# A recommendation kernel's dense layers moved to its start, and its last tile cut into four units of 32 samples

## The chip, the cores and the metric

The kernel runs on one NeuronCore of one Trainium2 chip. The metric is the device time of one execution in microseconds (us). The kernel is written engine by engine: TensorE (PE), VectorE (DVE), ScalarE (ACT), GpSimd (POOL) and SyncE (SP) each have a program of their own, in the order in which it is written, and meet only at semaphores.

## What is computed

For 2048 samples, 26 embedding rows of 64 floats and one dense feature are multiplied pairwise; the 351 products and a small network on the price feed a top layer of 256 units and one output.

```python
emb = emb_tables[jnp.arange(NUM_FIELDS)[:, None], x_cat]        # 26 x 2048 rows of 64
emb = jnp.transpose(emb, (1, 0, 2))
dense_embed = price[:, None] @ Wp + bp
feats = jnp.concatenate([emb, dense_embed[:, None, :]], axis=1)  # 27 features
gram = jnp.einsum('bid,bjd->bij', feats, feats)
interactions = gram[:, _IU, _JU]
h = jax.nn.relu(dense_embed @ W1 + b1)
dense_out = jax.nn.relu(h @ W2 + b2)
concat = jnp.concatenate([interactions, dense_out], axis=1)
t = jax.nn.relu(concat @ Wt1 + bt1)
out = (t @ Wt2 + bt2)[:, 0]
```

Everything is float32.

## The kernel before

The samples are cut into 16 tiles of 128. For each tile POOL issues 26 gathers (`gather`, L200), one for each field: each fetches 128 rows of 256 bytes into `gathered`, which has room for one tile, so that a gather of tile t+1 into a chunk of the columns waits until PE has transposed that chunk of tile t (`chunk_transposed`). There are two chunks, of 14 and 12 fields.

PE transposes pairs of fields into `ps_trans` (`transpose_fields`, L419). DVE and ACT copy the halves into `feats` (`evacuate_chunk`, L151), 64 samples on the upper 64 partitions and 64 on the lower. The products of four samples at a time are one matmul of 128 columns (`gram_matmuls`, L456), issued for both halves in turn; a tile has 32 of them, in two rounds of 16. DVE and ACT copy out of `ps_gram` what is wanted of a round (`evacuate_gram`, L141), 8 copies each. Where the profile counts instructions, each of these float32 matmuls and its weight load is two.

Tiles form batches: four of four tiles at most, here (0,4), (4,8), (8,12), (12,14), (14,15), (15,16). At the first tile of a batch PE also does the two dense layers for it (`hidden_layer` L441, `dense_out_layer` L446), and the top layer of the batch before (`top_layer`): for each of its two halves m one matmul from `dense_out` (L479) and seven from `gram` (L487), then the score (`score`, L495).

The last tile has transposes in four chunks of fields, (0,8), (8,16), (16,24), (24,26), and products in four rounds of eight matmuls. Its indices are laid out so that the first two rounds need only the first two chunks and the other two need all. After the last gather there come thus one transpose, its copies, two rounds of products, their copies, and the top layer of 128 samples. `keep_warm` (L402) issues matmuls whose result nobody reads, while PE waits.

The order of work is the order in which each engine's program is written: PE's last steps are `transpose_last`, `gram_last`, `top_layer`, `score`. An instruction that waits holds up all that is written behind it on the same engine.

Of the kernel before, what the change touches and what calls it, by code (L numbers as in the profile page):

```python
# [7 lines left out]
BM1, BM2, TM1 = 128, 64, 256  # L8
P = 128
# [6 lines left out]
UNITS = 2  # L16
UNIT = HALF // UNITS
# [9 lines left out]
LAST_CHUNKS = [(0, 8), (8, 16), (16, 24), (24, 26)]  # L27
LAST_ROUNDS = 4
LAST_RG = GROUPS // LAST_ROUNDS

BATCHES = [(0, 4), (4, 8), (8, 12), (12, 14), (14, 15), (15, 16)]
# [3 lines left out]
WARM = (0, 7, 3, 1, 1)  # L35
TO_GRAM, TO_TOP = 4, 5
# [9 lines left out]
def rec_kernel(nc, price, x_cat, table, consts, w1, w2, wt1_pairs, wt1_dense, out):  # L46
# [3 lines left out]
    with ExitStack() as ctx:  # L50
# [12 lines left out]
        last_base = sb("last_base", [P, FIELDS], i32)  # L63
# [11 lines left out]
        dense = sb("dense", [D, WIDE * P])  # L75
        hidden = sb("hidden", [BM1, WIDE * P])
        dense_out = sb("dense_out", [BM2, WIDE * P])
# [25 lines left out]
        last_gathered = [sem(f"last_gathered{c}") for c in range(len(LAST_CHUNKS))]  # L103
        chunk_transposed = [sem(f"chunk_transposed{c}") for c in range(NC)]
        last_transposed = sem("last_transposed")
# [12 lines left out]
        top_made = sem("top_made")  # L118
# [8 lines left out]
        last_from = ps_gram[:, :].rearrange("p (r h g s j c) -> p r h g s j c", r=2, h=2, g=LAST_RG, s=GROUP,  # L127
# [5 lines left out]

        def evacuate_gram(copy, t, r, quads):

            n = batch_of[t]
            rg = LAST_RG if t == LAST else RG
            source = last_from[:, r % 2] if t == LAST else gram_from
            for s in quads:
                for c in range(GROUP):  # L140
                    last = copy(gram_to[QUAD * c:QUAD * (c + 1), n % 2, t - BATCHES[n][0], :, rg * r:rg * (r + 1), :, s],  # L141
                                source[QUAD * s:QUAD * (s + 1), :, :, s, 0:SLABS, c])
            return last
# [10 lines left out]
        def evacuate_unit_chunk(copy, c, kk):  # L154

            f0, f1 = LAST_CHUNKS[c]
            src = ps_trans[:, BANK * (c % 2):BANK * (c % 2 + 1)].rearrange("p (m q h b) -> p m q h b", m=BANK // P, q=2, h=2)
            for u in range(UNITS):
                slots = [s for s in range(f0 + kk, f1, 2) if s // (FIELDS // 2) == u]
                if not slots:  # L160
                    continue
                m0, n, f = (slots[0] - f0) // 2, len(slots), 1 + 2 * (slots[0] % (FIELDS // 2))
                for h in range(2):
                    dst = feats[D * h:D * (h + 1), UNIT * u:UNIT * (u + 1), f:f + 4 * n]
                    dst = dst.rearrange("p b (m r) -> p m r b", r=4)[:, :, 0:2, :]
                    last = copy(dst, src[D * kk:D * (kk + 1), m0:m0 + n, :, h, :])  # L166
            return last

# [3 lines left out]
        def _(sp):  # L172
# [5 lines left out]
            sp.wait_ge(score_stored, len(BATCHES))  # L178
# [4 lines left out]
        def _(pool):  # L183

            pool.iota(field_base[:, :], pattern=[[VOCAB, FIELDS]], base=0, channel_multiplier=0).then_inc(base_made, 1)

            for q in range(2):

                pool.wait_ge(base_made, q + 1)
                pool.iota(last_base[HALF * q:HALF * (q + 1), :], pattern=[[0, UNITS], [2 * VOCAB, FIELDS // 2]],  # L190
                          base=q * VOCAB, channel_multiplier=0).then_inc(base_made, 1)
            pool.wait_ge(base_made, 3)
# [11 lines left out]
            for t in range(LAST):  # L204
                if t == 0:
                    pool.wait_ge(rows_made, 1)
                else:
                    pool.wait_ge(rows_made, 3)
# [379 lines left out]
```

## Time and profile before

| | |
|---|---|
| median of 3 runs | 541.97 us (541.65 to 544.13) |
| the profiled execution: time | 542.15 us |
| the profiled execution: span, first to last instruction | 540.3 us |
| POOL busy | 393.8 us, 73% of the span |
| PE busy | 246.3 us, 46% |
| ACT busy | 169.1 us, 31% |
| DVE busy | 145.4 us, 27% |
| mean granted TensorE clock | 0.70 of full speed |

The profiled execution is 0.18 us longer than the median; 1.85 us of its time lie outside the span. Busy time of POOL is that of the gathers' own instructions; between two of them lies a part that the profile calls "issue", in which the engine waits for nothing that the profile shows. The granted clock is 1.0 or 0.5 of 2.4 GHz in any stretch, so a number between them is a mean over both.

### The profile page before, as it was taken

Reading aid. Unit: us, or ns where it says so; the run is one execution under the profiler, and the core shown is the slowest. Engines: PE = TensorE matmul, PEld = TensorE weight load, DVE = VectorE, ACT = ScalarE, POOL = GpSimd, SP = SyncE. Lnnn points to the kernel's source line nnn. Section 1 sums busy time; section 2 is a strip of 40 time slices with the busy share of each in tenths; the row PEclk is TensorE's granted clock in tenths of the full one; section 3 lists DMA queues with packets and bytes.
Section 4 is the critical chain, followed back from the end, with each engine's and each line's share of the span. In section 5 each row is a group of like instructions: output and inputs, shape, how many; then the busy total and the mean of one; then the engine's idle time right before and its main releaser. Section 6 shows DMA issues by size and latency. Waiting matters only on the chain.

```text
span 540.3 us, 4362 instructions
## 1 busy us (share of the span) xinstructions
PE 246.3 (46%) x1496; PEld 177.9 (33%) x1496; DVE 145.4 (27%) x358; ACT 169.1 (31%) x405; POOL 393.8 (73%) x425
## 2 busy tenths in 40 slices
PE   0118033240569515134249733315136960565775
PEld 0105033240534304133234423305134440544654
DVE  3003233040331504123040331503233051333353
ACT  0124323041241604223042440503224052243563
POOL 6777777777777777777777777777777777777750
PEclk9999665555659856555577975755555985669798
DMA  6233333333323333333333333333332333332210
GB/s 187 26 26 27 26 28 27 26 27 27 26 27 27 26 27 28 26 26 27 26 29 26 27 27 26 27 27 27 26 27 26 26 28 26 26 28 27 28 22 2
DMA packets 14360, 16.26 MB, mean 30 GB/s; under 512 B 7169, under 2 KB 7425, under 8 KB 14209
## 3 DMA queue, kind: packets, MB, share of 16 engines
q0 software_dynamic: 13312, 13.66, 30.9%
q1 hardware_dynamic: 578, 2.19, 1.1%
q8 instruction: 12, 0.20, 0.1%
q10 hardware_dynamic: 448, 0.14, 0.1%
q14 instruction: 10, 0.08, 0.0%
HBM read 15.95 MB, written 0.01 MB: 30 GB/s over the span
## 4 chain that ended last, share of the span: by engine, by line
POOL 68%; issue 26%; DMA 2%; PE 2%; ACT 1%; DVE 0%; POOLq 0%
POOL gathered L200 68%; DMA gathered<-in_table,row_idx 2%; PE ps_mlp L487 1%; ACT gram L141 1%; PE ps_trans L419 1%; DMA raw_idx<-in_x_cat 0%; POOLq L50 0%; PE ps_gram L456 0%; PE ps_mlp L479 0%; PE ps_mlp L495 0%; DVE feats L166 0%; DVE top L368 0%; ACT scores L279 0%; DVE row_idx L339 0%; DVE wrapped L332 0%
## 5 line engine op out<-in xcount | busy, mean ns | idle before, releaser
L200 POOL DMA_INDIRECT gathered<-in_table,row_idx x416 | 392.7, 944 | 128.0 <-issue 125.9
L419 PE MATMUL ps_trans<-ident,gathered 128*128 128x128 f32 x208 | 45.4, 381 | 223.0 <-DMA gathered<-in_table,row_idx 223.0
L456 PE MATMUL ps_gram<-feats 64*128 64x128 f32 x1024 | 105.2, 384 | 61.0 <-ACT gram L141 30.2
L141 ACT COPY gram<-ps_gram 32x112 f32<-32x112 f32 (+1 forms) x272 | 97.2, 357 | 108.1 <-PE ps_gram L456 105.2
L141 DVE COPY gram<-ps_gram 32x112 f32<-32x112 f32 (+1 forms) x272 | 96.6, 355 | 116.8 <-PE ps_gram L456 113.5
L456 PEld LDWEIGHTS ps_gram<-feats 64*128 64x128 f32 x1024 | 96.9, 286 | 75.4 <-issue 52.6
L419 PEld LDWEIGHTS ps_trans<-ident,gathered 128*128 128x128 f32 x208 | 35.0, 198 | 236.3 <-issue 234.9
L151 ACT COPY feats<-ps_trans 64x448 f32<-64x448 f32 (+1 forms) x60 | 34.1, 569 | 195.4 <-PE ps_trans L419 195.0
L151 DVE COPY feats<-ps_trans 64x448 f32<-64x448 f32 (+1 forms) x60 | 36.8, 613 | 203.3 <-PE ps_trans L419 202.7
L487 PE MATMUL ps_mlp<-gram,wt1p_sb 128*128 128x512 f32 (+2 forms) x168 | 60.2, 520 | 2.9 <-ACT gram L141 2.9
L487 PEld LDWEIGHTS ps_mlp<-gram,wt1p_sb 128*128 128x128 f32 x168 | 32.6, 228 | 32.6 <-issue 28.0
L368 DVE TENSOR_SCALAR top<-ps_mlp,consts_sb 128x512 f32<-128x512 f32 (+2 forms) x6 | 3.4, 574 | 66.7 <-PE ps_mlp L487 66.7
L237 ACT ACTIVATE feats<-price_bc,consts_sb 64x64 f32<-64x64 f32 x32 | 15.6, 488 | 0.7
L479 PE MATMUL ps_mlp<-dense_out,wt1d_sb 64*128 64x512 f32 (+2 forms) x24 | 13.9, 672 | 2.0 <-ACT dense_out L269 2.0
L274 ACT ACTIVATE top<-ps_mlp,consts_sb 128x512 f32<-128x512 f32 (+2 forms) x6 | 3.3, 545 | 27.0 <-PE ps_mlp L487 27.0
L151 ACT ACT_TABLE_LOAD x1 | 1.3, 1283 | 25.4 <-PE ps_trans L419 25.4
L495 PE MATMUL ps_mlp<-top,consts_sb 128*1 128x512 f32 (+2 forms) x24 | 7.9, 449 | 1.0 <-DVE top L368 1.0
L479 PEld LDWEIGHTS ps_mlp<-dense_out,wt1d_sb 64*128 64x128 f32 x24 | 4.8, 247 | 6.7 <-issue 4.4
L446 PE MATMUL ps_mlp<-hidden,w_sb 128*64 128x512 f32 (+2 forms) x12 | 6.6, 644 | 0.5 <-ACT hidden L264 0.5
L441 PE MATMUL ps_mlp<-dense,w_sb 64*128 64x512 f32 (+2 forms) x12 | 5.4, 532 | 1.5 <-ACT scores L279 1.5
L402 PE MATMUL ps_trans<-wt1p_sb,ident 128*128 128x256 f32 x24 | 6.1, 388 | 0.0
L166 ACT COPY feats<-ps_trans 64x256 f32<-64x256 f32 (+2 forms) x10 | 4.5, 450 | 4.5 <-PE ps_trans L419 4.4
(24 smaller groups left out, 33.5 us busy)
## 6 DMA issues: line engine op xcount, KB each, us to landing
gathered<-in_table,row_idx POOLq DMA_INDIRECT x416, 3.3
price_bc<-in_price SPq DMA_DIRECT2D x1, 1024.0 KB, 5.2
wt1p_sb<-in_wt_pairs SPq DMA_DIRECT2D x1, 896.0 KB, 7.8
raw_idx<-in_x_cat SPq DMA_DIRECT2D x1, 195.0 KB, 2.7
w_sb<-in_w ACTq DMA_DIRECT2D x2, 32.0 KB, 4.8
wt1d_sb<-in_wt_dense ACTq DMA_DIRECT2D x1, 64.0 KB, 7.7
raw_idx<-in_x_cat SPq DMA_DIRECT2D x1, 13.0 KB, 1.8
consts_sb<-in_consts ACTq DMA_DIRECT2D x1, 4.5 KB, 2.0
```

Of the source, the lines that this page charges most:

```text
L141: last = copy(gram_to[QUAD * c:QUAD * (c + 1), n % 2, t - BATCHES[n][0], :, rg * r:rg * (r + 1), :, s], source[QUAD * s:QUAD * (s + 1), :, ...
L151: last = copy(feats[D * h:D * (h + 1), :, 1 + f0 + q:f1 + q:2], src[D * q:D * (q + 1), h, :, :])
L200: pool.indirect_dma_start(out=gathered[:, to * D:(to + 1) * D], out_offset=None, in_=rows, in_offset=bass.IndirectOffsetOnAxis(ap=row_idx[ ...
L237: return nc.scalar.activation(dst, price_bc[part, first:first + n], ACT.Identity, bias=const(BP, part), scale=const(WP, part))
L402: nc.tensor.matmul(ps_trans[:, BANK * bank:BANK * bank + TM1], ident[:, :], wt1p_sb[:, 0:TM1], start=True, stop=True)
L419: last = nc.tensor.transpose(ps_trans[:, to + k * P:to + (k + 1) * P], gathered[:, base + f * D:base + (f + 2) * D], ident[:, :])
L441: nc.tensor.matmul(ps_mlp[0][:, 0:width(n)], w1_sb[:, :], dense[:, 0:width(n)], start=True, stop=True)\
L446: nc.tensor.matmul(ps_mlp[1][0:BM2, 0:width(n)], w2_sb[:, :], hidden[:, 0:width(n)], start=True, stop=True)\
L456: last = nc.tensor.matmul(ps_gram[:, out_at:out_at + P], group, group, start=True, stop=True)
L479: nc.tensor.matmul(ps_mlp[m][:, 0:w], wt1d_sb[:, m * P:(m + 1) * P], dense_out[:, 0:w], start=True, stop=False)
L487: last = nc.tensor.matmul(ps_mlp[m][:, 0:w], wt1p_sb[:, j * TM1 + m * P:j * TM1 + (m + 1) * P], gram[:, at:at + w], start=False, stop=(j = ...
L495: last = nc.tensor.matmul(ps_mlp[0][0:1, 0:width(n)], const(WT2 + m), top[m][:, 0:width(n)], start=(m == 0), stop=(m == 1))
```

## The change

- The two dense layers are computed for all 2048 samples ahead of tile 0, in four steps of 512 columns, into a `dense_out` that now holds them all.
- The batches are (0,4), (4,8), (8,12), (12,14), (14,16). Tile 14 has its products in four rounds of eight matmuls.
- The last tile is gathered in four units of 32 samples and all 26 fields, in place of chunks of fields. A gather still fetches 128 rows; it now takes four fields for 32 samples (six such gathers a unit), and two further gathers carry the last two fields of two units each. So a unit has 7, 6, 7 and 6 gathers. Its transposes, copies and round of products follow unit by unit.
- The top layer of the last batch (256 columns) is in two parts: 224 columns (`EARLY`) that don't need the last unit, and 32 columns that do and that sum in `ps_trans`. The two sums of 224 columns are written before and after the last unit.
- There are 2 and 6 `keep_warm` matmuls before the second and third unit, none after; before there were 7, 3, 1 and 1.
- The base row numbers of the last tile are no longer made by POOL; DVE makes the last tile's indices in 12 small additions, in place of one.

```diff
-BATCHES = [(0, 4), (4, 8), (8, 12), (12, 14), (14, 15), (15, 16)]
+BATCHES = [(0, 4), (4, 8), (8, 12), (12, 14), (14, 16)]
+DENSE = BATCH // BANK
...
-WARM = (0, 7, 3, 1, 1)
+WARM = (2, 6, 0)
...
+        def last_part(m, late):
+
+            if not late:
+                return slice(0, EARLY), ps_mlp[m][:, 0:EARLY]
+            return slice(EARLY, 2 * P), ps_trans[:, BANK * m:BANK * m + UNIT]
...
+            pool.wait_ge(rows_made, 2 + 3 * UNITS)
             pool.wait_ge(chunk_transposed[0], LAST)
-            for c, (f0, f1) in enumerate(LAST_CHUNKS):
-                if c == 1:
+            for n in range(UNITS):
+                if n == 2:
                     pool.wait_ge(chunk_transposed[1], LAST)
-                for f in range(f0, f1):
-                    gather(LAST, f, last_gathered[c])
+                for col in UNIT_COLS[n]:
+                    gather(LAST, col, unit_gathered[n])
...
+            for q in range(UNITS):
+                part = slice(UNIT * q, UNIT * (q + 1))
...
+            def even_unit(n):
+                dve.wait_ge(unit_transposed, n + 1)
+                if n % 2 == 0:
+                    evacuate_shared(nc.vector.tensor_copy, n)
+                evacuate_unit(nc.vector.tensor_copy, n, 0).then_inc(trans_evac_dve, 1)
...
+            def top_sums(n, m, part, to, rounds):
+
+                a, first = BATCHES[n][0] * P, (n % 2) * SLABS * WIDE * P
+                nc.tensor.matmul(to, wt1d_sb[:, m * P:(m + 1) * P], dense_out[:, a + part.start:a + part.stop],
+                                 start=True, stop=False)
+                wait_gram_evac(rounds)
+                for j in range(SLABS):
+                    at = first + j * WIDE * P
+                    last = nc.tensor.matmul(to, wt1p_sb[:, j * TM1 + m * P:j * TM1 + (m + 1) * P],
+                                            gram[:, at + part.start:at + part.stop], start=False, stop=(j == SLABS - 1))
+                last.then_inc(top_summed[m], 1)
...
+            transpose_unit(0)
+            transpose_unit(1)
+            fine_round(LAST, 0)
+            fine_round(LAST, 1)
+            transpose_unit(2)
+            fine_round(LAST, 2)
+            top_part(0, 0)
+            transpose_unit(3)
+            fine_round(LAST, 3)
+            top_part(1, 0)
+            for m in range(2):
+                top_part(m, 1)
+            for late in range(2):
+                score_part(late)
```

PE's program at its end, before, from the transposes of fields 16 to 23 of the last tile on (L419 transposes, L402 `keep_warm`, L456 products, L479 and L487 top layer, L495 score; a matmul is counted once here):

```order
L419 MATMUL ps_trans<-ident,gathered 128x128 x4
L402 MATMUL ps_trans<-wt1p_sb,ident 128x256 x3
L419 MATMUL ps_trans<-ident,gathered 128x128
L402 MATMUL ps_trans<-wt1p_sb,ident 128x256
L456 MATMUL ps_gram<-feats 128x128 x16
L479 MATMUL ps_mlp<-dense_out,wt1d_sb 128x128
L402 MATMUL ps_trans<-wt1p_sb,ident 128x256
L487 MATMUL ps_mlp<-gram,wt1p_sb 128x128 x7
L479 MATMUL ps_mlp<-dense_out,wt1d_sb 128x128
L487 MATMUL ps_mlp<-gram,wt1p_sb 128x128 x7
L495 MATMUL ps_mlp<-top,consts_sb 1x128 x2
```

And now, from the third unit's product round on (L491 transposes, L538 products, L544 and L549 top layer, L579 score):

```order
L538 MATMUL ps_gram<-feats 128x128 x8
L544 MATMUL ps_mlp<-dense_out,wt1d_sb 128x224
L549 MATMUL ps_mlp<-gram,wt1p_sb 128x224 x7
L491 MATMUL ps_trans<-ident,gathered 128x128 x3
L538 MATMUL ps_gram<-feats 128x128 x8
L544 MATMUL ps_mlp<-dense_out,wt1d_sb 128x224
L549 MATMUL ps_mlp<-gram,wt1p_sb 128x224 x7
L544 MATMUL ps_trans<-dense_out,wt1d_sb 128x32
L549 MATMUL ps_trans<-gram,wt1p_sb 128x32 x7
L544 MATMUL ps_trans<-dense_out,wt1d_sb 128x32
L549 MATMUL ps_trans<-gram,wt1p_sb 128x32 x7
L579 MATMUL ps_mlp<-top,consts_sb 1x224 x2
```

One product round of eight stands behind the last transposes in place of two, and one half of the wide top layer stands ahead of them; behind the last products there are now three groups of top-layer matmuls and a fourth of the same kind, in place of two, and two scores in place of one.

ACT's program at its start, before (L237 makes dense features, L151 copies tile 0's transposes, L264 and L269 are the dense layers' rectifiers):

```order
L151 COPY feats<-ps_trans 64x64x7 x2
L237 ACTIVATE dense<-price_bc,consts_sb 64x512
L237 ACTIVATE feats<-price_bc,consts_sb 64x64 x2
L151 COPY feats<-ps_trans 64x64x6 x2
L141 COPY gram<-ps_gram 32x2x8x7 x8
L264 ACTIVATE hidden<-ps_mlp,consts_sb 128x512
L141 COPY gram<-ps_gram 32x2x8x7 x8
L269 ACTIVATE dense_out<-ps_mlp,consts_sb 64x512
```

And now (L258 dense features, L291 and L295 the rectifiers, L166 the copies of tile 0's transposes):

```order
L258 ACTIVATE dense<-price_bc,consts_sb 64x512
L291 ACTIVATE hidden<-ps_mlp,consts_sb 128x512
L258 ACTIVATE dense<-price_bc,consts_sb 64x512
L295 ACTIVATE dense_out<-ps_mlp,consts_sb 64x512
L291 ACTIVATE hidden<-ps_mlp,consts_sb 128x512
L258 ACTIVATE dense<-price_bc,consts_sb 64x512
L295 ACTIVATE dense_out<-ps_mlp,consts_sb 64x512
L291 ACTIVATE hidden<-ps_mlp,consts_sb 128x512
L258 ACTIVATE dense<-price_bc,consts_sb 64x512
L295 ACTIVATE dense_out<-ps_mlp,consts_sb 64x512
L291 ACTIVATE hidden<-ps_mlp,consts_sb 128x512
L295 ACTIVATE dense_out<-ps_mlp,consts_sb 64x512
```

All four steps of the dense layers now precede the first copy of tile 0.

## Rows read from the trace of the kernel before

**Rows 1.** The page: two groups of instructions; busy us, mean ns, idle before, releaser.

```profile
L200 POOL DMA_INDIRECT gathered<-in_table,row_idx x416 | 392.7, 944 | 128.0 <-issue 125.9
...
L151 ACT ACT_TABLE_LOAD x1 | 1.3, 1283 | 25.4 <-PE ps_trans L419 25.4
```

**Rows 2.** Timeline, the start: start, duration (us), instruction, idle before it.

```profile
3.71 1.11 POOL L200 DMA_INDIRECT gathered<-in_table,row_idx  x1 [1.56 <-DVE row_idx L339]
...
5.80 0.18 DVE L348 TENSOR_TENSOR row_idx<-clamped,last_base 128x26 uint32<-128x26 f32 x1
6.35 1.76 DVE L350 MEMSET feats<- 128x2048 f32 x1 [0.37 <-issue]
...
23.61 1.73 PE L419 MATMUL ps_trans<-ident,gathered 128*128 128x128 f32 x7 [23.61 <-DMA gathered<-in_table,row_idx]
...
41.46 3.78 PE L456 MATMUL ps_gram<-feats 64*128 64x128 f32 x32 [1.30 <-DVE feats L151]
45.03 1.91 PE L441 MATMUL ps_mlp<-dense,w_sb 64*128 64x512 f32 x2
...
48.45 0.69 ACT L264 ACTIVATE hidden<-ps_mlp,consts_sb 128x512 f32<-128x512 f32 x1
```

**Rows 3.** Timeline of the tail, from the last gathers to the end.

```profile
514.43 0.94 POOL L200 DMA_INDIRECT gathered<-in_table,row_idx  x1 [0.30 <-issue]
...
521.92 0.94 POOL L200 DMA_INDIRECT gathered<-in_table,row_idx  x1 [0.30 <-issue]
...
522.18 0.66 PE L419 MATMUL ps_trans<-ident,gathered 128*128 128x128 f32 x4
...
522.87 1.25 DVE L166 COPY feats<-ps_trans 64x256 f32<-64x256 f32 x2 [0.41 <-PE ps_trans L419]
...
524.78 0.33 PE L419 MATMUL ps_trans<-ident,gathered 128*128 128x128 f32 x1 [0.65 <-DMA gathered<-in_table,row_idx]
...
525.79 2.06 PE L456 MATMUL ps_gram<-feats 64*128 64x128 f32 x32 [0.25 <-DVE feats L166]
526.99 4.41 DVE L141 COPY gram<-ps_gram 32x56 f32<-32x56 f32 x16 [1.30 <-PE ps_gram L456]
...
527.54 0.30 PEld L479 LDWEIGHTS ps_mlp<-dense_out,wt1d_sb 64*128 64x128 f32 x2
...
531.56 2.64 PE L487 MATMUL ps_mlp<-gram,wt1p_sb 128*128 128x128 f32 x14 [2.89 <-ACT gram L141]
...
534.85 2.23 PE L487 MATMUL ps_mlp<-gram,wt1p_sb 128*128 128x128 f32 x14
...
537.53 0.60 PE L495 MATMUL ps_mlp<-top,consts_sb 128*1 128x128 f32 x4 [0.45 <-DVE top L368]
538.16 0.36 ACT L279 ACTIVATE scores<-ps_mlp,consts_sb 1x128 f32<-1x128 f32 x1 [3.56 <-PE ps_mlp L495]
```

**Rows 4.** Groups by shape: busy us, mean ns of one.

```profile
L166 DVE COPY feats<-ps_trans 64x192 f32<-64x192 f32 x2 | 1.0, 484 | 0.1
L166 DVE COPY feats<-ps_trans 64x64 f32<-64x64 f32 x4 | 1.1, 266 | 1.1 <-PE ps_trans L419 1.0
```

**Rows 5.** Timeline at 480 to 490 us: a top layer of 256 columns.

```profile
480.94 5.04 PE L487 MATMUL ps_mlp<-gram,wt1p_sb 128*128 128x256 f32 x14
...
486.54 3.29 PE L487 MATMUL ps_mlp<-gram,wt1p_sb 128*128 128x256 f32 x14
```

**Rows 6.** Stretches: us, PE, PEld, DVE, ACT, POOL busy, PEclk, DMA share, GB/s.

```profile
478.00:484.00 6.00, 5.87 (x16) 4.38 (x17) 1.26 (x2) 2.63 (x5) 4.54 (x5) 0.50 0.35 30
484.50:490.00 5.50, 5.33 (x23) 3.83 (x21) 0.14 (x1) 0.47 (x1) 4.28 (x5) 1.00 0.38 28
...
528.00:530.00 2.00, 0.67 (x3) 0.26 (x2) 1.88 (x9) 1.90 (x9) 0.00 (x0) 1.00 0.00 0
...
532.50:535.50 3.00, 3.00 (x13) 2.55 (x13) 0.00 (x0) 0.37 (x1) 0.00 (x0) 0.50 0.00 0
```

**Rows 7.** Weight loads at 527.3 to 527.9 us, by shape: busy us, mean ns.

```profile
L479 PEld LDWEIGHTS ps_mlp<-dense_out,wt1d_sb 64*128 64x128 f32 x2 | 0.3, 188 | 0.0
```

More of the change, by code:

```diff
@@ L274, in top_relu, with part_relu @@
                 nc.scalar.activation(top[0][:, 0:width(n)], ps_mlp[0][:, 0:width(n)], ACT.Relu, bias=const(BT1))\
-                    .then_inc(top_made, 1)
+                    .then_inc(top_made[0], 1)
+            def part_relu(late):
+                part, sums = last_part(0, late)
+                act.wait_ge(top_summed[0], last_batch + 1 + late)
+                nc.scalar.activation(top[0][:, part], sums, ACT.Relu, bias=const(BT1)).then_inc(top_made[0], 1)
             def store_scores(n):
@@ L280, in store_scores, with store_part @@
                                      ACT.Identity, bias=const(BT2, slice(0, 1))).then_inc(score_stored, 1)
+            def store_part(late):
+                part, _ = last_part(0, late)
+                first = BATCHES[last_batch][0] * P
+                act.wait_ge(score_summed, last_batch + 1 + late)
+                nc.scalar.activation(scores[:, first + part.start:first + part.stop],
+                                     ps_mlp[late][0:1, 0:part.stop - part.start],
+                                     ACT.Identity, bias=const(BT2, slice(0, 1))).then_inc(score_stored, 1)
@@ L282, in _ @@
+            dense_batch(0)
+            for k in range(DENSE):
+                hidden_relu(k)
+                if k + 1 < DENSE:
+                    dense_batch(k + 1)
+                dense_out_relu(k)
             for t in range(LAST):
                 n = batch_of[t]
-                first = t == BATCHES[n][0]
+                first = t == BATCHES[n][0] and n > 0
                 odd_fields(0, t)
+                dense_slots(t)
                 if first:
-                    dense_batch(n)
@@ L497, in score, with score_part @@
                 last.then_inc(score_summed, 1)
+            def score_part(late):
+                part, _ = last_part(0, late)
+                for m in range(2):
+                    pe.wait_ge(top_made[m], last_batch + 1 + late)
+                    last = nc.tensor.matmul(ps_mlp[late][0:1, 0:part.stop - part.start], const(WT2 + m), top[m][:, part],
+                                            start=(m == 0), stop=(m == 1))
+                last.then_inc(score_summed, 1)
+            for k in range(DENSE):
+                hidden_layer(k)
+                dense_out_layer(k)
@@ L528, in _ @@
-            top_layer(n)
-            score(n)
+                if t < LAST - 1:
+                    gram_round(t, 0)
+                    gram_round(t, 1)
+                else:
+                    for r in range(FINE_ROUNDS):
+                        fine_round(t, r)
+            transpose_unit(0)
[6 more added lines that the diff above has]
+            transpose_unit(3)
@@ L567 @@
     idx = cat.transpose(2, 1, 0).copy()
[L568 removed]
+    last = cat[:, -1].reshape(FIELDS, UNITS, 2, SIDE)
+    own = last[:SHARED].reshape(COLS, UNITS, UNITS, 2, SIDE).transpose(1, 3, 4, 2, 0).reshape(P, UNITS, COLS)
+    shared = last[SHARED:].reshape(2, 2, 2, 2, SIDE).transpose(2, 0, 3, 4, 1).reshape(P, 2)
+    for n in range(UNITS):
+        idx[:, -1, UNIT_COLS[n][0]:UNIT_COLS[n][0] + COLS] = own[:, n]
+        if n % 2 == 0:
+            idx[:, -1, UNIT_COLS[n][COLS]] = shared[:, n // 2]
     idx = idx.reshape(P, TILES * FIELDS)
```

319 lines of the change are left out of this document (162 added, 157 removed).

## The prediction

> **What bounds the kernel now.** I read the chain that ended last, which runs through POOL's gathers for nearly the whole span, and then their group on the page: 392.7 us busy and 125.9 us of "issue" ahead of the 416 gathers, out of 128.0 us idle [rows 1]. Of the 2.1 us that are left, 1.56 are the wait ahead of the first one [rows 2]. So POOL never waits for another engine in a way that counts: the first gather starts at 3.71, the last at 521.92 [rows 2, 3], which is 518.21 us over 415 steps, 1.249 us each. No work of the other engines inside that stretch costs anything unless it holds up a gather.
>
> Then I read the tail. The last data are there when PE starts the last transpose, at 524.78, 2.86 us after the last gather's start. From there to the end of the span, 540.3, are 15.5 us, and they are one chain: copies, two product rounds of eight from 525.79, their copies from 526.99 for 4.41 us, the top layer's two sums from 531.56 and 534.85, scores, the store [rows 3]. The reader should see in these rows that PE, DVE and ACT take turns. This tail is what the change can alter.
>
> The third view is the granted clock. PE was busy 0.67 of the 2.0 us from 528, then steadily from 531.56, and the clock reads 0.50 in 532.5 to 535.5. The other way round, it was busy 5.87 of 6 us at 0.50, and then the clock reads 1.00 [rows 6]. These two levels are 1.2 and 2.4 GHz.
>
> **What stays.** There are 416 gathers before and after, each of 128 rows; I take 1.249 us for each. The first waits for the same DVE result. Hence the last data again at 524.8.
>
> **The dense layers at the start.** ACT begins them when `feats` is zeroed. The twelve additions stand ahead of that; the one that they replace took 0.18 us, and at as much each the memset of 1.76 us starts near 8.3 instead of 6.35, and ends at 10.1 [rows 2]. Then the table load, 1.3 us [rows 1], and one activation, some 0.8. A step is two matmuls of 1.91 us, a rectifier of 0.69 and two more matmuls that I take at the same 1.9 [rows 2]: 4.5 us, four of them 18.0. That ends at 30.2. The transposes of tile 0 stood at 23.61 and took 1.73 us; they move to about 30.2 and end at 31.9. The first gather that needs them is the 27th, at 3.71 + 26 x 1.249 = 36.2. There are 4.3 us in hand, so the cost is nothing. Beyond 36.2 each us would be a us of the total. Their removal from later tiles, from between product rounds, gains nothing either, as POOL is the bound there.
>
> **Tile 14 in four rounds.** Its copies are four rounds of eight copies an engine at 4.41/16 = 0.276 us [rows 3], 8.8 us. They must be done before those of the second unit, whose last gather is 13 steps, 16.2 us, behind that of tile 14. That cover holds with 7 us to spare. No POOL wait hangs on it.
>
> **The third unit.** Its last gather is the one of 514.43, six steps ahead of the last [rows 3]; with 2.86 us its data are there at 517.3. The six `keep_warm` matmuls ahead of it take 12/14 of 3.29, 2.8 us, at the upper level and twice that at the lower [rows 5]; in the second case they may end some 0.7 us late. Four transposes until the copies start: 0.69 (522.18 to 522.87) [rows 3]. DVE has two copies of 64 x 64 and two of 64 x 192, 2 x 0.266 + 2 x 0.484 = 1.5 us [rows 4], plus 0.1 to hand over: 519.6. The new copies have inner runs of 16 in place of 32; I take the same time by element count, between the 0.38 and 0.62 of the neighbouring sizes. One product round of eight until its copies start is 1.20 us (525.79 to 526.99) [rows 3] at the upper level; sixteen took 3.78 at the lower [rows 2], so eight are about 2.1. Eight copies, 2.2, and 0.15 to hand over. So the first wide sum (`top_part(0, 0)`) can start its seven products with `gram` at 523.15, or 524.05 at the lower level.
>
> **Its place is what costs.** This sum stands ahead of the last unit's transposes on PE, and behind it wait those transposes, the copies, the last round and everything to the end. Fourteen instructions of 256 columns took 3.29 us at the upper level; without the 0.3 that the last one drains, and times 224/256, that is 2.6 us, and 5.2 at half of the clock. The row of 5.04 us [rows 5] is mixed, since the clock rose in its course [rows 6]. So the last transposes start at 523.15 + 2.6 = 525.75 at best and at 524.05 + 5.2 = 529.25 at worst, against data at 524.8: 1.0 to 4.5 us late.
>
> **From the last transposes to the end**, at the upper level. Three transposes until the copies start 0.6, two copies 0.97, handing over 0.1. The round of eight holds PE 0.9 (2.06 for two, less the drain). The second wide sum has sixteen instructions, 16/14 of 2.6, plus 0.1: 3.1. The last round's copies (1.2 after its start, 2.2 long) end within it, at no cost. Then two narrow sums of sixteen instructions. A matmul of 32 columns needs little, but each has its own weight load: two loads take 0.30 us together [rows 3] where one takes 0.188 [rows 7], so one every 0.11 us. That is 1.8 and 0.1 each, 3.8. Next the score of 224 columns, four instructions at 0.19: 0.75; drain and handing over 0.3; ACT's store of 224 and then of 32 scores 0.43 + 0.27, estimated around the 0.36 for 128; and 1.78 from there to the end (540.3 less 538.52) [rows 3]. Sum: 1.67 + 0.9 + 3.1 + 3.8 + 0.75 + 0.3 + 0.7 + 1.78 = 13.0.
>
> On the weight loads a page is weighed. The row shows 14 instructions of 256 columns with a load of 128 columns each in 3.29 us, 0.235 apart [rows 5]; had the 0.11 of load been added to the streaming, the streaming of 256 columns would be 0.125, and 128 columns half of it, whereas the one-column weights of the score take 0.60 us for four of 128 columns, 0.15 each [rows 3]. The loads overlap. The Trainium skill ("TensorE: Matmul & The Clock Gate", Part 3, The mechanism) says that a load overlaps a matmul in flight only where the row groups differ, which would speak against many narrow sums. By it the 32 narrow instructions would cost 0.03 more each, an estimate from the streaming time, 0.9 us in all; I go by the row.
>
> **The likeliest case (0.46).** From 515 to 523 PE has little to do: 0.5 us of transposes, a round of products, and waits. That is like the stretch from 528 on, after which the clock was 0.50. So I take the third unit's round at the lower level, 0.9 more, and a part of the wide sum, 1.0 of its possible 2.6. Last transposes at 525.75 + 1.9 = 527.65, end at 527.65 + 13.0 = 540.65, which is 0.35 over the span before. On the median, 541.97 + 0.35 = 542.3. The own range of this case is 541.6 to 543.2. I gain a product round's copies (2.2) and an amount of streaming, and give them back in the late start and in the second pair of sums.
>
> **The rivals.** (B, 0.22) The upper level holds nearly throughout: 525.75 + 13.0 = 538.75, 1.55 less; 540.4. For it speak the six warming matmuls ahead of unit three; against it the idle time behind them.
>
> (C, 0.23) The lower level holds for all of the round and the wide sum, then rises: 529.25 + 13.0 = 542.25, 1.95 more; 543.9. The steady work of the wide sum is at its end by then, which is the state in which the clock rose before [rows 6]. By the Trainium skill (same page, Part 1) the throttled level is the default and activity has to lift it; that would bring this case and not B.
>
> (D, 0.06) Slower by more than 0.5%. The place is the work behind the last transposes: if the lower level stays there too, the 9.0 us that are PE's (0.45 transposes, 0.9, 3.1, 3.8, 0.75) double, 551.3, in time 552.9. It decides once the end passes 543.0: from 542.25 that is 1.5 us more at the lower level. Against it: PE works almost without a pause there.
>
> (E, 0.03) Faster by more than 0.5%: the narrow matmuls aren't held by their loads but take 0.03 us each, as by their 32 columns; 32 x 0.08 = 2.6 less than B, 537.8. Against it the loads' row.
>
> **How the numbers follow.** A measurement of this kernel can tell about 0.5%, 2.7 us, from no change. A, B and C all lie inside: same 0.91. Faster is E, 0.03; slower is D, 0.06, in which a start that holds up the 27th gather is contained. The predicted time is A's, 542.3. The range reaches to B and a little beyond C, 540.2 to 544.2.
>
> **What would show it.** Gathers 1.249 us apart without a gap at 36 us, the last near 521.9; PE through with the dense layers near 30. The wide sum ahead of the last transposes, which start between 525.7 and 529 though the data came at 524.8. Behind the last products the wide sum of 3.1 us, two narrow ones of 1.8 each, copies of the last round hidden. Wrong I would be if the copies of the new shape took clearly over 0.5 us, if the last unit's transposes started at 524.8, if the narrow matmuls were not 0.11 us apart, or if the clock stayed at 0.50 past 530.

## The result, and the profile after

| | before | after |
|---|---|---|
| median of 13 runs | 541.89 us (540.91 to 544.13) | 544.70 us (543.84 to 545.23) |
| span of the profiled execution | 540.3 us | 543.0 us |
| mean granted TensorE clock | 0.70 | 0.72 |

The ratio is 1.0048, with a 95% interval of 1.0037 to 1.0059: the kernel became slower by a little under 0.5%. The forecast was 542.3 us and a range up to 544.2.

The start went as forecast. The chain that ended last, from its view in order of time (start, duration, what), shows the end of the dense layers and tile 0's transposes:

```profile
25.95 2.02 PE ps_mlp L501 x2
28.73 1.97 PE ps_mlp L507 x2
30.70 1.70 PE ps_trans L473 x7
```

The transposes end at 32.4, against 31.9 in the prediction, and the 27th gather is due near 36.2. POOL's waits (us in total, times, longest) show that it wasn't held up. None of the seven waits put down to PE is longer than the 0.3 us of issue that stand ahead of any gather:

```profile
POOL gathered L220 <- issue: 124.4, 408, 0.3
...
POOL gathered L220 <- PE ps_trans L473: 2.1, 7, 0.3
```

The tail is where the time went. The timeline, from the third unit's transposes on, answers to [rows 3]:

```profile
518.09 0.55 PE L491 MATMUL ps_trans<-ident,gathered 128*128 128x128 f32 x3 [0.93 <-DMA gathered<-in_table,row_idx]
...
520.35 1.16 PE L538 MATMUL ps_gram<-feats 64*128 64x128 f32 x16 [1.59 <-DVE feats L176]
521.34 0.54 PE L544 MATMUL ps_mlp<-dense_out,wt1d_sb 64*128 64x224 f32 x2
...
521.56 2.17 DVE L152 COPY gram<-ps_gram 32x56 f32<-32x56 f32 x8 [1.26 <-PE ps_gram L538]
...
522.84 0.94 POOL L220 DMA_INDIRECT gathered<-in_table,row_idx  x1 [0.30 <-issue]
523.88 5.25 PE L549 MATMUL ps_mlp<-gram,wt1p_sb 128*128 128x224 f32 x14 [2.00 <-ACT gram L152]
528.97 0.49 PE L491 MATMUL ps_trans<-ident,gathered 128*128 128x128 f32 x3
...
529.50 0.96 DVE L176 COPY feats<-ps_trans 64x192 f32<-64x192 f32 x2 [5.78 <-PE ps_trans L491]
...
530.57 1.16 PE L538 MATMUL ps_gram<-feats 64*128 64x128 f32 x16 [1.10 <-DVE feats L176]
...
532.00 2.92 PE L549 MATMUL ps_mlp<-gram,wt1p_sb 128*128 128x224 f32 x14
...
535.18 1.75 PE L549 MATMUL ps_trans<-gram,wt1p_sb 128*128 128x32 f32 x14
...
537.20 1.75 PE L549 MATMUL ps_trans<-gram,wt1p_sb 128*128 128x32 f32 x14
538.88 1.85 PE L579 MATMUL ps_mlp<-top,consts_sb 128*1 128x224 f32 x8
...
540.55 0.61 ACT L317 ACTIVATE scores<-ps_mlp,consts_sb 1x224 f32<-1x224 f32 x2 [3.29 <-PE ps_mlp L579]
```

The row to look at is the one at 523.88. The first wide sum takes 5.25 us, where the same fourteen instructions at 532.00 take 2.92. The last transposes start only when it is through, at 528.97. Their gather was issued at 522.84; with the 2.86 us of before, the data were there at 525.7. So they are 3.3 us late. From them to the end are 14.0 us. The stretches (us, busy of PE, PEld, DVE, ACT and POOL, granted clock, DMA share, GB/s) show why the two sums differ:

```profile
515.00:518.00 3.00, 2.16 (x10) 1.52 (x8) 1.37 (x6) 1.38 (x6) 2.08 (x4) 0.99 0.17 22
518.00:521.00 3.00, 1.32 (x14) 1.05 (x16) 1.46 (x4) 0.96 (x2) 2.39 (x3) 1.00 0.13 31
521.00:524.00 3.00, 1.00 (x13) 0.68 (x9) 2.07 (x8) 2.10 (x8) 2.17 (x3) 0.64 0.16 24
524.00:527.00 3.00, 3.00 (x9) 2.71 (x9) 0.00 (x0) 0.00 (x0) 0.00 (x0) 0.50 0.08 11
527.00:530.00 3.00, 2.46 (x10) 2.03 (x8) 0.49 (x2) 0.49 (x2) 0.00 (x0) 0.72 0.00 0
530.00:533.00 3.00, 2.43 (x23) 2.19 (x24) 1.64 (x6) 2.10 (x7) 0.00 (x0) 1.00 0.00 0
```

PE is busy 1.32 and then 1.00 of 3 us between 518 and 524. The clock falls in that stretch, and the wide sum runs at 0.50, the level of 1.2 GHz. It is back at 1.00 from 530 on, and falls once more before the scores, this time though PE was busy without a pause:

```profile
535.00:540.00 5.00, 5.00 (x36) 4.11 (x37) 0.66 (x2) 0.29 (x1) 0.00 (x0) 0.89 0.01 3
540.00:543.00 3.00, 0.73 (x6) 0.30 (x4) 0.00 (x0) 0.61 (x2) 0.00 (x0) 0.50 0.01 3
```

Of the 2.7 us between the spans, 0.92 lie ahead of all this, since the last gather was issued at 522.84 and not 521.92. The experiments below show that this part belongs to the one execution: in `after_d` the last gather is at 521.93.

### The profile page after: what moved, and what is told of

It is laid out like the page before. It is cut to its first block, busy times and chain, and to the rows that moved or that the text cites. A ratio compares the mean times of both kernels' runs of the same rounds, so it can differ in the third digit from the quotient of the medians.

```text
span 543.0 us, 4380 instructions
## 1 busy us (share of the span) xinstructions
PE 256.8 (47%) x1481; PEld 182.4 (34%) x1481; DVE 150.1 (28%) x387; ACT 170.2 (31%) x413; POOL 394.3 (73%) x423
## 4 chain that ended last, share of the span: by engine, by line
POOL 60%; issue 23%; PE 8%; DMA 5%; ACT 1%; DVE 1%; POOLq 0%; SPq 0%; ACTq 0%
POOL gathered L220 60%; DMA gathered<-in_table,row_idx 4%; PE ps_trans L473 2%; PE ps_mlp L501 1%; PE ps_mlp L549 1%; PE ps_mlp L507 1%; PE ps_trans L549 1%; ACT hidden L291 1%; DMA raw_idx<-in_x_cat 0%; PE ps_gram L538 0%; ACT gram L152 0%; DVE feats L176 0%; DVE feats L396 0%; PE ps_mlp L579 0%; ACT L258 0%
## 5 line engine op out<-in xcount | busy, mean ns | idle before, releaser
L517 PE MATMUL ps_gram<-feats 64*128 64x128 f32 x896 | 96.6, 399 | 61.4 <-ACT gram L157 43.7
L157 ACT COPY gram<-ps_gram 32x112 f32<-32x112 f32 x224 | 83.6, 373 | 103.7 <-PE ps_gram L517 101.4
L517 PEld LDWEIGHTS ps_gram<-feats 64*128 64x128 f32 x896 | 89.9, 302 | 71.5 <-issue 50.2
L157 DVE COPY gram<-ps_gram 32x112 f32<-32x112 f32 x224 | 83.1, 371 | 106.0 <-PE ps_gram L517 103.3
L166 ACT COPY feats<-ps_trans 64x448 f32<-64x448 f32 (+1 forms) x60 | 34.1, 569 | 194.2 <-PE ps_trans L473 193.9
L166 DVE COPY feats<-ps_trans 64x448 f32<-64x448 f32 (+1 forms) x60 | 36.7, 612 | 202.3 <-PE ps_trans L473 201.9
L549 PE MATMUL ps_mlp<-gram,wt1p_sb 128*128 128x512 f32 (+2 forms) x140 | 58.9, 581 | 2.0 <-ACT gram L152 2.0
L549 PEld LDWEIGHTS ps_mlp<-gram,wt1p_sb 128*128 128x128 f32 x140 | 30.7, 226 | 32.1 <-issue 28.4
L416 DVE TENSOR_SCALAR top<-ps_mlp,consts_sb 128x512 f32<-128x512 f32 (+1 forms) x4 | 2.7, 684 | 56.0 <-PE ps_mlp L549 56.0
L258 ACT ACTIVATE feats<-price_bc,consts_sb 64x64 f32<-64x64 f32 x30 | 14.7, 490 | 0.8
L501 PE MATMUL ps_mlp<-dense,w_sb 64*128 64x512 f32 x8 | 8.3, 1134 | 11.7 <-ACT dense L258 11.7
L538 PE MATMUL ps_gram<-feats 64*128 64x128 f32 x128 | 11.2, 334 | 5.3 <-DVE feats L176 2.7
L544 PE MATMUL ps_mlp<-dense_out,wt1d_sb 64*128 64x512 f32 (+2 forms) x20 | 12.6, 718 | 0.0
L538 PEld LDWEIGHTS ps_gram<-feats 64*128 64x128 f32 x128 | 10.1, 239 | 7.3 <-issue 3.3
L300 ACT ACTIVATE top<-ps_mlp,consts_sb 128x512 f32<-128x512 f32 (+1 forms) x4 | 2.5, 634 | 26.2 <-PE ps_mlp L549 26.2
L152 ACT COPY gram<-ps_gram 32x56 f32<-32x56 f32 x32 | 8.5, 264 | 4.0 <-PE ps_gram L538 3.6
L152 DVE COPY gram<-ps_gram 32x56 f32<-32x56 f32 x32 | 8.4, 262 | 4.0 <-PE ps_gram L538 3.6
L507 PE MATMUL ps_mlp<-hidden,w_sb 128*64 128x512 f32 x8 | 7.9, 1086 | 3.1 <-ACT hidden L291 3.1
L154 DVE COPY gram<-ps_gram 32x56 f32<-32x56 f32 x32 | 8.3, 259 | 2.9 <-PE ps_gram L538 2.4
```

The costliest lines, as they stand in the source:

```text
L152: last = copy(gram_unit[to, w, k, r, :, :, :, s], fine_from[part, r % 2, :, :, s, 0:SLABS, c])
L157: last = copy(gram_to[to, w, k, :, RG * r:RG * (r + 1), :, s], gram_from[part, :, :, s, 0:SLABS, c])
L166: last = copy(feats[D * h:D * (h + 1), :, 1 + f0 + q:f1 + q:2], src[D * q:D * (q + 1), h, :, :])
L258: return nc.scalar.activation(dst, price_bc[part, first:first + n], ACT.Identity, bias=const(BP, part), scale=const(WP, part))
L501: nc.tensor.matmul(ps_mlp[0][:, :], w1_sb[:, :], dense[:, :], start=True, stop=True).then_inc(hidden_summed, 1)
L507: nc.tensor.matmul(ps_mlp[1][0:BM2, :], w2_sb[:, :], hidden[:, :], start=True, stop=True)\
```

## The experiments

The theory is that two things together make the loss. The first wide sum stands ahead of the last transposes on PE, and the clock has fallen when it starts. The rivals are that the place alone costs, that the dense layers at the start cost, and that the program slows the gathers. Runs that were made together share the runs of the kernel before.

| run | what it is | median us | ratio to before, 95% interval |
|---|---|---|---|
| `after_d` | changed kernel | 544.60 | 1.0038 (1.0024 to 1.0052) |
| `warm_sum_b` | seven more warming matmuls | 542.10 | 0.9991 (0.9971 to 1.0012) |
| `sum_behind_b` | first wide sum behind the last round | 545.65 | 1.0072 (1.0046 to 1.0097) |
| `dense_first` | kernel before, dense layers at its start | 542.05 | 1.0003 (0.9985 to 1.0022) |
| `split192` | parts of 192 and 64, three more warming | 539.14 | 0.9951 (0.9929 to 0.9973) |
| `split192_plain_b` | parts of 192 and 64 | 539.07 | 0.9955 (0.9937 to 0.9973) |
| `split192_warm_b` | parts of 192 and 64, eight more warming | 538.24 | 0.9925 (0.9909 to 0.9942) |

Each trace shows one execution, and the executions of one kernel differ. The 31 of the kernel before that belong to `warm_sum_b` lie in three groups: 9 at 540.3 to 540.9 us, 12 at 541.8 to 542.6, 10 at 543.5 to 544.2. `split192_plain_b` has five at 538.3 to 539.1 and four at 540.8 to 541.3. The changed kernel keeps closer together, with all of its 25 (the first result and `after_d`) at 542.8 to 545.2. What makes the groups isn't shown.

Seven other runs were made on two occasions on which the kernel before takes about 660 us: 663.2 beside the first four (`before_again`, `after_again`, `warm_sum`, `sum_behind`), 659.2 beside the other three. They are told first, since they settle one rival and leave the others open by their times.

### The gathers' steps: before_again, after_again

`before_again` is the kernel before and `after_again` the changed one, both without an edit.

> The kernel before, unchanged, to see whether its gathers keep their 1.2487 us spacing on another occasion. In the changed kernel they were 1.2508 us apart, uniformly from the second tile on, which put the last gather at 522.84 in place of 521.92. If the spacing belongs to the chip and not to the program, this run and the three beside it have one spacing, whichever it is. If it belongs to the program, this one has 1.2487 and the other three 1.2508.

> The changed kernel, unchanged, as the reference for the runs beside it. Theory (the wide sum of 224 columns runs at the lower clock and holds the last transposes up): last transposes about 3.3 us behind the data, ratio to before about 1.005. Rival (0.9 of the 2.8 us are the chip's gather spacing): ratio nearer 1.003 here, as both kernels then have the same spacing.

`before_again` took 665.41 us in its one run. `after_again` took 662.29, 0.9998 of the kernel before there (0.9961 to 1.0035), below both ratios that I had named. The group of gathers on the pages of the two kernels on this occasion, `before_again` first (busy us, mean ns, idle before):

```profile
L200 POOL DMA_INDIRECT gathered<-in_table,row_idx x416 | 393.6, 946 | 226.1 <-issue 121.0 <-PE ps_trans L419 91.0 <-remote 12.5
```

```profile
L220 POOL DMA_INDIRECT gathered<-in_table,row_idx x416 | 392.6, 944 | 225.5 <-issue 120.7 <-PE ps_trans L473 73.8 <-remote 28.8
```

The two figures have changed sides. The kernel before has 946 ns a gather here and the changed one 944; in the first pair of profiles it was 944 [rows 1] and 946. The profile of `after_d` has 944 as well. So the 2 ns, which make 0.9 us over 416 gathers, go with the execution and not with the program, and this rival falls. I had named two outcomes, one step for all four runs made together or one for each program; neither came. `sum_behind`, beside them, has 944 and `warm_sum` 947.

Both kernels' POOL waits some 100 us more here, most of it for transposes. I took the cause to be data that come late, and say so in expectations below; the trace of `before_again` doesn't bear it out. The copies of tile 0's first products wait for PE alone, and the products were through by 46 us:

```profile
41.52 3.79 PE L456 MATMUL ps_gram<-feats 64*128 64x128 f32 x32 [1.30 <-issue]
...
76.93 3.12 ACT L141 COPY gram<-ps_gram 32x112 f32<-32x112 f32 x8 [35.63 <-remote]
```

So engines stand still although their inputs are made; what releases them so late isn't shown. The times are spread wide as well, 658.2 to 675.3 us for the kernel before on the first occasion. Five first tries of runs that are told below were made on these two occasions. Their edits are given there; this was expected of them:

`warm_sum`:

> Seven more warming matmuls: three between the third unit's transposes and its round, four between the first matmul of the wide sum and its wait for the copies. Theory (the lost time is the clock's): the wide sum's fourteen instructions take 2.9 in place of 5.2 us, the last transposes start 1 us behind their data in place of 3.3, and the time falls by 2.3 us against the changed kernel, to that of the kernel before. Rival (the place alone costs, or the clock doesn't rise for such work): no change, or a few tenths slower, if the warming matmuls push the round back.

`sum_behind`:

> The first wide sum stands behind the last product round, beside the second. Theory: the last transposes start when their data come (3.3 us earlier than in the changed kernel), and 2.9 us of a wide sum at the upper level, or 5.2 at the lower, are added behind; so between 0.4 us faster and 1.9 us slower than the changed kernel. If the place were the whole cost, it would be 3.3 us faster.

`after_c`, the changed kernel:

> The changed kernel once more, for a second profile of its tail on an undisturbed chip. Theory: the first wide sum's fourteen instructions take between 4 and 5.3 us again and the last transposes start 2 us or more behind their data; ratio to before 1.003 to 1.006. The steps between gathers are 1.249 or 1.251 us, whichever the execution has. Rival (the first profile was an outlier and the clock is mostly high there): 2.9 us and a ratio of 1.000.

`split192_plain`:

> The parts of 192 and 64 columns without the three added warming matmuls, so that only the order of the work differs from the changed kernel. Theory: the first wide sum in the former gap keeps PE at work and the second one has the time until the data come, at either level nearly; 0 to 1 us above the version with warming (539.1). Rival (the warming alone made that version fast, by the clock): 541.5 or more, as the second wide sum at the lower level, 4.5 us, holds the last transposes up by 2.

`split192_warm`:

> The version of 192 and 64 columns with five more warming matmuls, two between the last transposes and their round, three between the first matmul of the late sums and its wait for copies. Theory: the second late sum, which took 3.08 us as the clock fell during it, takes 1.75, and the last score 0.45 in place of 0.8: 1.0 to 1.7 us less, 537.5 to 538.1. Rival (the clock falls by its own phase anyway): 539.1.

| first try | median us | ratio to before, 95% interval |
|---|---|---|
| `warm_sum` | 660.92 | 0.9985 (0.9951 to 1.0018) |
| `sum_behind` | 661.57 | 0.9987 (0.9950 to 1.0024) |
| `after_c` | 661.56 | 1.0022 (0.9998 to 1.0047) |
| `split192_plain` | 658.68 | 0.9984 (0.9958 to 1.0010) |
| `split192_warm` | 658.11 | 0.9971 (0.9949 to 0.9993) |

Four of the five intervals contain 1, and they overlap too much to tell the theories apart, so each was run again. The traces do tell. The tail of `after_c` has the same slow wide sum:

```profile
639.60 5.14 PE L549 MATMUL ps_mlp<-gram,wt1p_sb 128*128 128x224 f32 x14 [1.99 <-ACT gram L152]
644.57 0.49 PE L491 MATMUL ps_trans<-ident,gathered 128*128 128x128 f32 x3
```

The tail of `warm_sum`, the same kernel with seven more warming matmuls, has the fast one:

```profile
643.61 2.89 PE L554 MATMUL ps_mlp<-gram,wt1p_sb 128*128 128x224 f32 x14
...
646.34 0.49 PE L495 MATMUL ps_trans<-ident,gathered 128*128 128x128 f32 x3
```

### The changed kernel again: after_d

> The changed kernel once more, for a second profile of its tail; the try before fell on a chip whose gathers land some 15 us later. Theory: the first wide sum's fourteen instructions take between 4 and 5.3 us again and the last transposes start 2 us or more behind their data; ratio to before 1.003 to 1.006. The steps between gathers are 1.249 or 1.251 us, whichever the execution has. Rival (the first profile was an outlier and the clock is mostly high there): 2.9 us and a ratio of 1.000.

The ratio is 1.0038. The timeline of the tail:

```profile
521.93 0.94 POOL L220 DMA_INDIRECT gathered<-in_table,row_idx  x1 [0.30 <-issue]
```

```profile
517.38 0.55 PE L491 MATMUL ps_trans<-ident,gathered 128*128 128x128 f32 x3 [1.90 <-DMA gathered<-in_table,row_idx]
...
519.62 2.08 PE L538 MATMUL ps_gram<-feats 64*128 64x128 f32 x16 [1.59 <-DVE feats L176]
...
524.13 5.53 PE L549 MATMUL ps_mlp<-gram,wt1p_sb 128*128 128x224 f32 x14 [1.69 <-ACT gram L152]
529.49 0.50 PE L491 MATMUL ps_trans<-ident,gathered 128*128 128x128 f32 x3
```

Here the last gather is where it was before, at 521.93, and yet the span is 543.2. The round at 519.62 is at the lower level too, 2.08 us in place of 1.16, and the last transposes are 4.7 us behind the data (521.93 + 2.86 = 524.8). The first profile was no outlier: in all four profiles of the changed kernel (the first, `after_again`, `after_c`, `after_d`) the wide sum took 5.14 to 5.56 us, which is the lower level from end to end, or nearly.

### More warming matmuls: warm_sum_b

```diff
+            def warm(count):
+                for _ in range(count):
+                    nc.tensor.matmul(ps_trans[:, BANK:BANK + TM1], ident[:, :], wt1p_sb[:, 0:TM1], start=True, stop=True)
...
                                  start=True, stop=False)
+                warm(extra)
                 wait_gram_evac(rounds)
...
             transpose_unit(2)
+            warm(3)
             fine_round(LAST, 2)
```

The lines behind the first cut stand in `top_sums`, behind its matmul from `dense_out`. `extra` is 4 in `top_part(0, 0)` and 0 elsewhere.

> Seven more warming matmuls: three between the third unit's transposes and its round, four between the first matmul of the wide sum and its wait for the copies; again, since in the first try on another chip the gathers' data came some 15 us late and hid the tail's order. Theory (the lost time is the clock's): the wide sum's fourteen instructions take 2.9 in place of 5.2 us, the last transposes start 1 us behind their data in place of 3.3, and the time is 2.3 us below the changed kernel's 544.7, about 542.4. Rival (the clock doesn't rise for such work, or the place alone costs): 544.7 or a few tenths more.

The median is 542.10 us, 2.5 us below `after_d` and level with the kernel before. The timeline and the stretches:

```profile
521.00 1.99 PE L461 MATMUL ps_trans<-wt1p_sb,ident 128*128 128x256 f32 x8
523.06 2.89 PE L554 MATMUL ps_mlp<-gram,wt1p_sb 128*128 128x224 f32 x14
525.79 0.49 PE L495 MATMUL ps_trans<-ident,gathered 128*128 128x128 f32 x3
```

```profile
518.00:521.00 3.00, 2.69 (x25) 1.93 (x23) 1.68 (x6) 1.18 (x4) 2.13 (x3) 1.00 0.12 22
521.00:524.00 3.00, 2.93 (x14) 2.40 (x14) 1.83 (x7) 1.85 (x7) 1.64 (x2) 1.00 0.21 32
524.00:527.00 3.00, 2.28 (x14) 1.99 (x12) 0.67 (x2) 0.68 (x2) 0.00 (x0) 1.00 0.00 1
```

PE is busy where it was idle, the clock stays at 1.00, and the wide sum takes 2.89 us. The last transposes start at 525.79, 3.7 us earlier than in `after_d`. The work added is of no other use, and both traces of this version have 2.89 us where all four of the changed kernel have 5.14 to 5.56; so the clock is shown as the cause of the loss. This execution is the prediction's case of the upper level up to the last transposes, 525.75 forecast and 525.79 measured. Its span is 539.7 and not 538.75, since the stretch behind them is 0.9 longer than forecast here too. The twelve executions lie between 540.6 and 543.7; the traced one, at 541.56, is among the shorter ones.

### The first wide sum behind the last round: sum_behind_b

```diff
-            top_part(0, 0)
             transpose_unit(3)
             fine_round(LAST, 3)
+            top_part(0, 0)
             top_part(1, 0)
```

On ACT `gram_round(3, t)` stands ahead of `part_relu(0)`.

> The first wide sum stands behind the last product round, beside the second; again, for the same reason. Theory: the last transposes start with their data, 3.3 us earlier, and 2.9 us (upper level) or 5.2 us (lower) of a wide sum are added behind: 544.3 to 546.6. If the place were the whole cost: 541.4.

```profile
524.71 0.87 PE L491 MATMUL ps_trans<-ident,gathered 128*128 128x128 f32 x3 [3.03 <-DMA gathered<-in_table,row_idx]
...
526.68 2.08 PE L538 MATMUL ps_gram<-feats 64*128 64x128 f32 x16 [1.10 <-DVE feats L176]
...
529.41 4.17 PE L549 MATMUL ps_mlp<-gram,wt1p_sb 128*128 128x224 f32 x14
```

The transposes start as soon as their data come, at 524.71, and the kernel is slower still, 545.65 us; all eight executions lie above all 25 of the changed kernel. The stretch had even less work for PE, so the transposes, the round and most of the sum are at the lower level. Moving the sum away saves its wait and adds its length behind; the place alone is not the cost.

### The dense layers alone: dense_first

The kernel before with the changed kernel's `dense_batch`, `hidden_relu`, `dense_out_relu`, `hidden_layer` and `dense_out_layer` ahead of tile 0, and nothing else of the change.

> The kernel before with its dense layers ahead of tile 0 for all samples, and nothing else of the change. Theory: POOL's 27th gather doesn't wait, the later tiles don't bound, and the tail loses only the dense matmuls among waits: the ratio to before is 1.000 within 0.001. Rival (this part brings the loss, by a stop of the gathers near 36 us or by later steps of 1.251 us): 1.002 to 1.004.

The ratio is 1.0003 (0.9985 to 1.0022). This part costs and brings nothing that can be told (0.8 us less to 1.2 us more lie inside the interval), as forecast.

### Another cut: split192, split192_plain_b, split192_warm_b

```diff
-EARLY = 2 * P - UNIT
+EARLY = 2 * P - 2 * UNIT
...
                 keep_warm(n, n % 2)
+                if n == 2:
+                    top_part(0, 0)
                 pe.wait_ge(unit_gathered[n], 16 * len(UNIT_COLS[n]))
...
             fine_round(LAST, 2)
-            top_part(0, 0)
+            top_part(1, 0)
             transpose_unit(3)
             fine_round(LAST, 3)
-            top_part(1, 0)
+            score_part(0)
             for m in range(2):
                 top_part(m, 1)
-            for late in range(2):
-                score_part(late)
+            score_part(1)
```

The early sums now wait for two product rounds only, and the rectifiers and stores on ACT and DVE move along. The cut is that of `split192_plain_b`. `split192` has three warming matmuls ahead of the third unit's round, `split192_plain_b` none, `split192_warm_b` the three, two ahead of the last round and three in the first late sum.

> The parts of the last top layer are 192 and 64 columns in place of 224 and 32. So the first wide sum needs only the rounds of the first two units and stands ahead of the third unit's transposes, the second one behind its product round; the score of the 192 columns stands ahead of the late sums; three warming matmuls are added ahead of the third unit's round. The narrow sums stay as long as now, 1.75 us each, since their weight loads set them: 64 columns stream in less than the 0.11 us of a load. Theory: nothing holds up the last transposes, and neither a wide sum nor a wide score is left behind them: they start within 1 us of their data, and the end is 8.5 us behind the late sums' start (3.7 for them, 0.6 score, 0.3 store, 1.8 to the end, 2.2 for the copies that are now bare), 538.5 to 540 in all, 0.4 to 0.6 percent faster than the kernel before. Rival (the 64 columns stream at the lower clock and set the pace, or the wide sums still hold the transposes up): 541 to 543.

> The parts of 192 and 64 columns without the three added warming matmuls, so that only the order of the work differs from the changed kernel; again, for the same reason. Theory: the second wide sum has the time until the data come, at either level nearly; 0 to 1 us above the version with warming (539.1). Rival (the warming alone made that version fast, by the clock): 541.5 or more, as the second wide sum at the lower level, 4.5 us, holds the last transposes up by 2.

> The version of 192 and 64 columns with five more warming matmuls, two between the last transposes and their round, three between the first matmul of the late sums and its wait for copies; again, for the same reason. Theory: the second late sum, which took 3.08 us as the clock fell during it, takes 1.75, and the last score 0.45 in place of 0.8: 1.0 to 1.7 us less, 537.5 to 538.1. Rival (the clock falls by its own phase anyway): 539.1.

All three have lower medians than both kernels, and intervals below 1: 539.14, 539.07 and 538.24 us, the last 0.75% below the kernel before. The tail of `split192_plain_b`:

```profile
516.11 2.54 PE L555 MATMUL ps_mlp<-gram,wt1p_sb 128*128 128x192 f32 x14
...
522.09 2.54 PE L555 MATMUL ps_mlp<-gram,wt1p_sb 128*128 128x192 f32 x14
...
524.61 0.52 PE L497 MATMUL ps_trans<-ident,gathered 128*128 128x128 f32 x3
...
529.77 1.75 PE L555 MATMUL ps_trans<-gram,wt1p_sb 128*128 128x64 f32 x14 [1.28 <-ACT gram L152]
...
531.81 2.27 PE L555 MATMUL ps_trans<-gram,wt1p_sb 128*128 128x64 f32 x14
```

Both wide sums now lie in time that PE had to spare, one ahead of the third unit and one behind it. Both take 2.54 us, at the upper level, with no added warming: the useful work keeps the clock up. It is so in the traces of all five runs of this cut, first tries included (2.51 to 2.54 us); the longer executions of `split192_plain_b` have no trace. The last transposes start at 524.61, and the wide sums are gone from behind them. I had given this version time at either level; it was the upper. The late sums of 64 columns take 1.75 us, exactly what 32 columns took in the changed kernel, so their weight loads, which are the same, pace them. A fixed step for each instruction is the rival. Against it stand the scores of `sum_behind_b`, with weights of one column and 32 streamed ones at the end: three of their loads pass in 0.14 us. What is left is the second late sum, 2.27 us, during which the clock falls (granted clock 0.73 in 532 to 534). In `split192_warm_b` it is

```profile
532.27 1.77 PE L556 MATMUL ps_trans<-gram,wt1p_sb 128*128 128x64 f32 x14
```

and the time is 0.9 us below `split192`, where 1.0 to 1.7 was expected, and 0.8 below `split192_plain_b`; its six executions lie below eight of the nine of the latter. I had worked from the 3.08 us which this sum took in the profile of `split192`. It varies: the first try `split192_plain` had 1.77 with no added warming, so one trace of each doesn't show how much of the 0.8 is this sum's. In the execution of `split192_warm_b` all from the first wide sum on stood 0.5 to 0.6 us later (last transposes at 525.11, not 524.61).

## Why the prediction was wrong

- **What bounds the kernel** was right: POOL is never held up beyond its 0.3 us of issue once it has begun, and only the tail decides. `dense_first` confirms it for the dense layers; in the first profile the PE work of the start ended 0.5 us later than worked out.
- **The third unit** was right in its sizes. The new copies with runs of 16 took 0.96 us for two, as the element count gave. The wide sum could start at 523.88 in the first profile (522.96 without the gathers' 0.92) and 524.13 in `after_d`; 523.15 to 524.05 was forecast, so the two lie 0.2 and 0.1 outside it.
- **Its place is what costs** was right as a mechanism, and both ends of its bound were met. From the start of the sum to the last transposes were 2.73 us at the upper level (`warm_sum_b`) and 5.09 and 5.36 at the lower; 2.6 and 5.2 was forecast.
- **The step that failed** is the choice between these ends in "The likeliest case": "a part of the wide sum, 1.0 of its possible 2.6". It was nearly all of it. From its start to the last transposes were 5.09 us in the first profile and 5.36 in `after_d`, where 3.6 was taken. The last transposes start at 528.05 in the first profile, without the gathers' 0.92, and at 529.49 in `after_d`, not at 527.65. The row of before showed the clock low for all of 532.5 to 535.5, while PE worked through a sum that it had begun after idle time. I had this, and still let the clock rise in the middle of the sum. Rival C, which I gave 0.23, had the transposes at 529.25; `after_d` is that case up to there.
- **From the last transposes to the end** is the second term that was too small. I had 13.0 us; they are 14.0 in the first profile, 13.7 in `after_d`. The second wide sum took 3.3 with its gaps, not 3.1, and the narrow sums 2.0 each, not 1.9. The scores were the larger miss: 1.7 us from the first of them to ACT's store (538.88 to 540.55), 1.4 in `after_d`, where 1.05 was taken. They ran at the lower level; in `sum_behind_b`, at the upper one, the same stretch is 0.95 us. I took the level to stay up behind steady work. It fell with PE busy all the time, behind the same narrow sums behind which it stayed up in `sum_behind_b`; why is open.
- **The sums.** For `after_d`: 540.65 + 1.84 for the transposes + 0.7 for the end = 543.2, the measured span. For the first profile: 540.65 + 0.4 for the transposes + 0.92 for the gathers + 1.0 for the end = 543.0. There the third unit's round had run at the upper level, 1.16 us where I took 0.9 more, so that the slow sum cost less on balance. The range's upper end, 544.2, was 0.3 over C's time, and the median of 544.7 lies beyond it, because C took the same 13.0 us for all that came behind.
- **On the weight loads** the row was right and not the rule weighed against it. By the Trainium skill ("TensorE: Matmul & The Clock Gate", Part 3, The mechanism) a load would not overlap a matmul with the same row groups. The sums of 32 and of 64 columns both take 1.75 us for fourteen. If load and streaming were added, the one with 64 columns would be the longer. The trace doesn't agree with the Trainium skill here.

## What to carry to other kernels

Work put into a gap ahead of late data is free only if it ends before the data come, at the clock that it finds there; size it with the duration at the lower level, if PE was mostly idle before it. Fill such a gap from its beginning, with the part of the sum that is already computable (192 of 256 columns here, in place of 224): the same work then keeps the clock up and is out of the way. A narrow sum isn't cheaper than one twice as wide while its weight loads pace it.

## What the runs showed of the hardware

- Fourteen instructions with weight loads of 128 columns take 1.75 us for 32 and for 64 streamed columns at the upper level, about 0.12 us each with the last one's drain.
- The gathers took 944 ns in some executions and 946 in others, of either kernel: 0.9 us in the total.
- On two occasions the kernel before took 663 and 659 us in place of 542, with POOL waiting about 100 us more. In `before_again` DVE and ACT began copies at 76.93 whose products were made by 46. Why is open. The record gives the second occasion the chip number 5, and the later runs under the same number took 542, so the number alone doesn't decide it.
- In the changed kernel the wide sum was at the lower level in each of four tails, whereas I had taken the level to be nearly open. With the idle time filled it was at the upper one in both tails.
- The clock also fell to 0.50 at the scores of the first profile, behind 5.00 of 5 us busy. A busy PE in the rows isn't enough to say that the level stays.
